# State-space statistics moved to ScalarE, whole products with B in a ring of three, five states weighed by GpSimd, and a multiplied mask

## The reference

```python
h = _layernorm(x) * (1 + ca) + sa
x = x + ga * attention(h)          # 16 heads of 16, causal, linear position bias
h = _layernorm(x) * (1 + cb) + sb
x = x + gb * fp4_ffn(h)            # 704 wide, silu(gate) * up, blocks of 16 rounded to FP4
# second layer, other mod rows
h = _layernorm(x) * (1 + ca) + sa
x = x + ga * state_space(h)
h = _layernorm(x) * (1 + cb) + sb
x = x + gb * experts(h)            # shared and routed low-rank experts
```

```python
xn = layernorm(x) * ln_w + ln_b
x_inner, z = split(xn @ W_in.T)
u = silu(causal_conv4(x_inner) + conv_b)
dt_low, B, C = split(u @ W_x.T)                     # 64, 16, 16
dt = clip(softplus(dt_low @ W_dt.T + b_dt) + DT_MIN, DT_MIN, DT_MAX)
h_t = exp(dt_t * A) * h_(t-1) + (dt_t * u_t) * B_t   # for each channel and state
y_t = sum over states of h_t * C_t, plus u_t * D_param
out = (y * silu(z)) @ W_out.T + x
```

## Time and profile before

| | |
|---|---|
| time before, median of 3 runs | 4210.48 us (4206.35 to 4210.94) |
| profiled execution | 4207.32 us, span 4205.4 us |
| DVE busy | 3592.4 us, 85% of the span |
| PE busy | 3374.6 us, 80% |
| POOL busy | 2620.3 us, 62% |
| ACT busy | 2249.4 us, 53% |

### The profile page before, as it was taken

The page is one execution under the profiler, slowest core; times in us unless marked ns, Lnnn a source line. Parts: engine busy times, 40 slices in busy tenths (PEclk is TensorE's granted clock), DMA queues, the critical chain, the costliest instruction groups (busy, mean ns, idle before and its releaser), DMA issues. The chain is left out here.

```text
span 4205.4 us, 60689 instructions
## 1 busy us (share of the span) xinstructions
PE 3374.6 (80%) x21452; PEld 1522.8 (36%) x21452; DVE 3592.4 (85%) x6348; ACT 2249.4 (53%) x3974; POOL 2620.3 (62%) x2515
## 2 busy tenths in 40 slices
PE   5979999999994999999567777777777777777467
PEld 3623333333332555565222222222222222222166
DVE  5768888888855999999289999999999999999966
ACT  5626666666672333333265665666665565665422
POOL 1102322222222888887188888988889898988823
PEclk8969999999996999999778887888888888887689
DMA  4884565656513111110112222222222222212122
GB/s 146 279 175 67 75 88 67 88 75 82 77 32 87 35 44 47 47 43 26 47 48 52 69 59 62 67 58 50 54 69 60 66 65 56 67 51 52 40 93 83
DMA packets 273931, 299.55 MB, mean 71 GB/s; under 512 B 34559, under 2 KB 204662, under 8 KB 273622
## 3 DMA queue, kind: packets, MB, share of 16 engines
q1 hardware_dynamic: 273630, 295.68, 31.7%
HBM read 210.22 MB, written 84.51 MB: 70 GB/s over the span
## 5 line engine op out<-in xcount | busy, mean ns | idle before, releaser
L1679 POOL TENSOR_TENSOR d_dBu<-d_dtu,d_Bn 128x1024 f32<-128x1024 f32 x512 | 1202.7, 2377 | 157.7 <-DVE d_h L1746 157.5
L1525 ACT ACTIVATE d_dA<-d_dt,d_decay 128x512 f32<-128x512 f32 x1024 | 688.6, 687 | 414.2 <-DVE d_h L1746 412.5
L745 ACT ACTIVATE b_P<-b_pT 128x512 f32<-128x512 f32 (+1 forms) x1120 | 571.4, 576 | 328.8 <-PE b_pT L653 328.5
L1746 DVE TENSOR_TENSOR_SCAN d_h<-d_dA,d_last_h,d_dBu 128x512 f32<-128x512 f32 x512 | 616.9, 1265 | 21.2 <-ACT d_dA L1525 18.2
L1746 DVE TENSOR_TENSOR_SCAN d_h<-d_dA,d_dBu 128x512 f32<-128x512 f32 x512 | 587.1, 1205 | 50.3 <-ACT d_dA L1525 47.9
L775 DVE CUSTOM_DVE_ANT_0 b_pS<-b_pS,mask_qk 128x512 f32<-128x512 f32 (+3 forms) x1024 | 581.2, 618 | 50.1 <-PE b_pS L663 45.1
L663 PE MATMUL b_pS<-KS,QS 99*128 99x512 bf16 (+3 forms) x1536 | 471.4, 339 | 71.7 <-DVE b_Gc L775 47.3
L625 POOL TENSOR_SCALAR_AFFINE_SELECT b_P<-b_P 128x128 f32<-128x128 f32 (+2 forms) x608 | 191.4, 321 | 506.1 <-ACT b_P L745 493.3
L653 PE MATMUL b_pT<-QS,KS 118*128 118x512 bf16 (+3 forms) x1536 | 450.1, 330 | 19.5 <-ACT b_gT L729 16.3
L1753 DVE TENSOR_TENSOR d_h<-d_h,d_C 128x2048 f32<-128x2048 f32 x192 | 434.6, 2263 | 0.5 <-PE d_C L1408 0.5
L1408 PE MATMUL d_C<-d_bc,d_pick 96*128 96x512 bf16 x256 | 118.0, 461 | 359.5 <-DVE d_h L1753 359.2
(11 more groups left out here) (300 smaller groups left out, 5906.5 us busy)
## 6 DMA issues: line engine op xcount, KB each, us to landing
d_Bn<-scratch_bs SPq DMA_DIRECT2D x64, 1024.0 KB, 8.2
scratch_parts<-a_part SPq DMA_DIRECT2D x48, 512.0 KB, 4.1
QS<-scratch_parts SPq DMA_DIRECT2D x192, 128.0 KB, 7.3
KS<-scratch_parts SPq DMA_DIRECT2D x192, 128.0 KB, 7.8
scratch_v<-a_v SPq DMA_DIRECT2D x16, 1024.0 KB, 7.6
V<-scratch_v SPq DMA_DIRECT2D x32, 512.0 KB, 11.7
a_x<-in_L_attn_x_dram SPq DMA_DIRECT2D x16, 512.0 KB, 7.6
scratch_o<-b_O SPq DMA_DIRECT2D x16, 512.0 KB, 10.2
```

The costliest lines, as they stand in the source:

```text
L745: act.activation(t[:, heads[0]:heads[-1] + 1, c * CH:c * CH + w], pT[:, place % RING, 0:len(heads) * w].rearrange("p (h w) -> p h w", w=w) ...
L1525: act.activation(dA[:, m % 2, :], dt[:, c.k % 2, m, :], ACT.Exp, scale=decay[:, m, n:n + 1]).then_inc(dA_d, 1)
L1679: pool.tensor_tensor(dBu[:, n % 2, 2 * j:2 * j + 2, :], dtu[:, c.k % 2, 2 * j:2 * j + 2, :], Bn[:, n // BG % 2, n % BG, :].unsqueeze(1).to ...
L1746: dve.tensor_tensor_scan(h[:, n % HS, m, :], dA[:, m % 2, :], dBu[:, n % 2, m, :], start, ALU.mult, ALU.add).then_inc(scanned, 1)
```

## The change

Four things change.

1. In `attend` the mask of the diagonal blocks is a multiply: the weights, read as 32-bit integers, times `cap`, an integer matrix of ones and zeros that `setup` makes once. The rows that keep the scores out of foreign blocks hold -1024 and no longer -1e30.
2. In `feed_forward` ACT takes the statistics of x2 in two more roles, `s_` and `v_`, 10 and 11 steps back: a Copy that sums, one element scaled to the negated mean over 16, and a Square that sums. They are kept for all 64 tiles, and SP's load of x waits for them besides.
3. In `state_space` the statistics of x by DVE and the four small operations of POOL for them are gone. POOL makes the factors of all 64 tiles at the start, in four operations of 128x64, behind the signal `set_up`. The second layer norm keeps its statistics.
4. POOL makes a product with B whole, 128x2048, into a ring of three states; it waits for all scans of state n-3, and DVE for the whole product. POOL weighs the states 0, 3, 6, 9, 12. B comes two states at a time, so there are 128 transfers of half the size, each as soon as the product two groups before has let its buffer go.

```diff
-                pool.affine_select(out=own, in_=own, compare_op=ALU.is_ge, fill=0.0,
-                                   base=0, pattern=[[0, len(heads)], [-1, P]], channel_multiplier=1).then_inc(p_masked, 1)
+                pool.tensor_tensor(own.bitcast(I32), own.bitcast(I32), K["cap"][:, :].unsqueeze(1).to_broadcast([P, len(heads), P]), ALU.mult).then_inc(p_masked, 1)
...
+                wait(sp, var_d, n.times(1, 1 - XS))
                 sp.dma_start(x[:, n.k % XS, :], xin[bass.ds(n.times(P), P), :]).then_inc(t_in[n.k % 4], 16)
...
+                if v_ is not None:
+                    n = v_.base * U + v_.k
+                    wait(act, sum_d, v_.times(1, 1))
+                    act.activation(K["x2_neg"][:, n:n + 1], x2_sum[:, n % 2, :], ACT.Copy, scale=-1.0 / (16.0 * D)).then_inc(neg_d, 1)
...
                     act.activation(he[:, h_.k % 2, :], he[:, h_.k % 2, :], ACT.Relu, bias=floor[:, :], scale=ROUND).then_inc(hm_d, 1)
+                if v_ is not None:
+                    n = v_.base * U + v_.k
+                    wait(act, neg_d, v_.times(1, 1))
+                    act.activation(unread[:, n % 2, :], x[:, n % XS, :], ACT.Square, bias=K["x2_neg"][:, n:n + 1], scale=1.0 / 16.0, accum_out=K["x2_var"][:, n:n + 1]).then_inc(var_d, 1)
+                if s_ is not None:
+                    n = s_.base * U + s_.k
+                    wait(act, x2_d, s_.times(1, 1))
+                    wait(act, var_d, s_.times(1, -1))
+                    act.activation(unread[:, n % 2, :], x[:, n % XS, :], ACT.Copy, accum_out=x2_sum[:, n % 2, :]).then_inc(sum_d, 1)
...
-POOL_C = (0, 4, 8, 12)
+POOL_C = (0, 3, 6, 9, 12)
...
-HS, BG = 4, 4
+HS, BG, BS = 4, 2, 3
...
+        def product(c, n):
+            return dBu[:, c.times(NS, n) % BS, :, :]
...
+            def spread_next(c, g):
+                if c is not None:
+                    wait(sp, dBu_d, c.times(NS, BG * (g - 1)))
+                    spread_b(c, g)
...
-                for j in range(2):
-                    wait(pool, scanned, c.times(NS * MD, MD * (n - 2) + 2 * j + 2))
-                    pool.tensor_tensor(dBu[:, n % 2, 2 * j:2 * j + 2, :], dtu[:, c.k % 2, 2 * j:2 * j + 2, :],
-                                       Bn[:, n // BG % 2, n % BG, :].unsqueeze(1).to_broadcast([P, 2, CH]), ALU.mult).then_inc(dBu_d, 1)
+                wait(pool, scanned, c.times(NS * MD, MD * (n + 1 - BS)))
+                pool.tensor_tensor(product(c, n), dtu[:, c.k % 2, :, :], Bn[:, n // BG % 2, n % BG, :].unsqueeze(1).to_broadcast([P, MD, CH]), ALU.mult).then_inc(dBu_d, 1)
                 if n - 2 in POOL_C:
                     weigh(c, n - 2)
...
+            pool.tensor_tensor(rstd_x[:, :], K["x2_var"][:, :], eps[:, :], ALU.add).then_inc(sx_step, 1)
+            pool.tensor_tensor(nmr_x[:, :], K["x2_neg"][:, :], sixteen[:, :], ALU.mult).then_inc(sx_step, 1)
+            pool.wait_ge(sx_step, 2)
+            pool.tensor_tensor(rstd_x[:, :], rstd_x[:, :], half[:, :], ALU.pow).then_inc(sx_step, 1)
+            pool.wait_ge(sx_step, 3)
+            pool.tensor_tensor(nmr_x[:, :], nmr_x[:, :], rstd_x[:, :], ALU.mult).then_inc(sx, 1)
...
-                ({15: finish}, {14: step_input}, {3: lambda f: scale_bias(f, 0), 6: shift, 8: lambda f: scale_bias(f, 1)}))
+                ({15: finish}, {14: step_input}, {6: shift, 8: scale_bias}))
...
+                wait(dve, dBu_d, c.times(NS, n + 1))
                 for m in range(MD):
-                    if m % 2 == 0:
-                        wait(dve, dBu_d, c.times(2 * NS, 2 * n + m // 2 + 1))
...
-                 {1: lambda f: stats(f, 0), 4: modulate, 6: lambda f: stats(f, 1), 13: carry}))
+                 {4: modulate, 6: stats, 13: carry}))
```

More of the change, by code:

```diff
@@ L31 @@
 MASKED = -1.0e30
+BELOW = -1024.0
+CAP = 1
 EPS = 1e-5
@@ L1038, in _, with step @@
             pe.wait_ge(w_in, 16)
-            def step(a, e, n_, d, b, h_, q, c, o_):
+            def step(a, e, n_, d, b, h_, q, c, o_, s_, v_):
                 if a is not None:
@@ L1389, in step @@
                 if f is not None and f.k % 2 == 0:
-                    wait_before(sp, x3_d, f.times(1, -2), passed)
+                    wait(sp, x3_d, f.times(1, -2))
                     sp.dma_start(mrow[:, f.k // 2 % 2, GA, :], S["mod"][bass.ds(f.over(2), 1), 1, GA, :].to_broadcast([P, D])).then_inc(g_in[f.k // 2 % 2], 16)
@@ L1555, in normalise @@
                 if 0 in tiles:
-                    wait(act, rs, f.times(2, j + 1))
-                    if j == 1:
+                    if j == 0:
+                        wait(act, sx, 1)
+                        wait(act, x_in, f.times(16, 16))
+                    else:
+                        wait(act, rs, f.times(1, 1))
                         wait(act, h_mul, f.times(1, 1))
@@ L1561, in normalise @@
                 for t in tiles:
-                    last = act.activation(x[:, t, :], src[:, t, :], ACT.Identity, bias=nmr[:, j, t:t + 1], scale=rstd[:, j, t:t + 1])
+                    n = (f.base * U + f.k) * CT + t
+                    bias, scale = (nmr_x[:, n:n + 1], rstd_x[:, n:n + 1]) if j == 0 else (nmr[:, t:t + 1], rstd[:, t:t + 1])
+                    last = act.activation(x[:, t, :], src[:, t, :], ACT.Identity, bias=bias, scale=scale)
                 if CT - 1 in tiles:
@@ new lines, in _, with scale_bias @@
+            pool.tensor_tensor(nmr_x[:, :], K["x2_neg"][:, :], sixteen[:, :], ALU.mult).then_inc(sx_step, 1)
[3 more added lines that the diff above has]
+            pool.tensor_tensor(nmr_x[:, :], nmr_x[:, :], rstd_x[:, :], ALU.mult).then_inc(sx, 1)
+            def scale_bias(f):
+                wait(pool, stat, f.times(2, 2))
+                wait(pool, xn2, f.times(1, 0))
+                pool.tensor_tensor(rstd[:, :], mv[:, :, 1], eps[:, 0:CT], ALU.add).then_inc(rs_step, 1)
+                pool.tensor_tensor(nmr[:, :], mv[:, :, 0], minus[:, :], ALU.mult).then_inc(rs_step, 1)
+                wait(pool, rs_step, f.times(3, 2))
+                pool.tensor_tensor(rstd[:, :], rstd[:, :], half[:, 0:CT], ALU.pow).then_inc(rs_step, 1)
+                wait(pool, rs_step, f.times(3, 3))
+                pool.tensor_tensor(nmr[:, :], nmr[:, :], rstd[:, :], ALU.mult).then_inc(rs, 1)
@@ L1712, in _ @@
             run(pool, unit,
-                ({15: finish}, {14: step_input}, {3: lambda f: scale_bias(f, 0), 6: shift, 8: lambda f: scale_bias(f, 1)}))
+                ({15: finish}, {14: step_input}, {6: shift, 8: scale_bias}))
         @block.vector
         def _(dve):
-            for t, value in ((half, -0.5), (eps, EPS), (minus, -1.0), (growth, GROWTH), (v_max, V_MAX)):
+            for t, value in ((half, -0.5), (eps, EPS), (minus, -1.0), (sixteen, 16.0), (growth, GROWTH), (v_max, V_MAX)):
                 dve.memset(t[:, :], value).then_inc(const, 1)
@@ L1740, in scan @@
                     wait(dve, last_put, c.over(2, NS, n + 1))
+                wait(dve, dBu_d, c.times(NS, n + 1))
                 for m in range(MD):
-                    if m % 2 == 0:
-                        wait(dve, dBu_d, c.times(2 * NS, 2 * n + m // 2 + 1))
                     wait(dve, dA_d, c.times(NS * MD, MD * n + m + 1))
                     start = 0.0 if c.k % 2 == 0 else last_h[:, n, m, :]
-                    dve.tensor_tensor_scan(h[:, n % HS, m, :], dA[:, m % 2, :], dBu[:, n % 2, m, :], start, ALU.mult, ALU.add).then_inc(scanned, 1)
+                    dve.tensor_tensor_scan(h[:, n % HS, m, :], dA[:, m % 2, :], product(c, n)[:, m, :], start, ALU.mult, ALU.add).then_inc(scanned, 1)
             def weigh(c, n):
@@ L1806, in gate_y @@
                 wait(dve, silu_z, e.times(1, 1))
-                wait(dve, dBu_d, e.times(2 * NS, 2 * NS))
+                wait(dve, dBu_d, e.times(NS, NS))
                 dve.tensor_tensor(dtu[:, e.k % 2, :, :], y[:, :, :], z[:, e.k % 2, :, :], ALU.mult).then_inc(yz_d, 1)
```

96 lines of the change are left out of this document (44 added, 52 removed).

## The result

The changed kernel takes 4281.68 us (median of 4 runs, 4279.11 to 4283.25) against 4208.73 us (4 runs) of the kernel before on the same chip: 1.0172 times as long, 95% interval 1.0159 to 1.0185. The prediction was 4270, range 4198 to 4330, slower with a chance of 0.73. The profiled execution took 4281.3 us with a span of 4279.6, that is 74.2 us more than the 4205.4 of before.

The account below looks back on a forecast made before the run. DVE was taken to set the pace of the state-space stage. To 4207.3 us came +33 for its chunks (+2.2 in each of 15), +8 for its head, +22 for the attention: 4270 us, range 4198 to 4330.

Parts of the forecast that it names:

- Attention, +22: Diagonal mask at key tile 3: the integer multiply, priced as float, delays PE about 0.7 us in 32 units, +22 us.
- the multiply costs what the select did: Rival for the attention's mask: the integer multiply is no dearer than the select, total 4248 us; chance 0.12.
- Feed-forward, 0: ACT's two added passes per tile, 1.1 us, lie under 1.6 us of cover before PE needs oT: no cost.
- Head, +8: Start of the state-space stage: the 64-column power takes 10.4 us in series, so the first scan comes 7.7 us later.
- State 3, 1.0 of the statistics' 1.73 comes back: Chunk's turn: without statistics DVE waits for ACT's decay behind PE's convolution, losing 1.0 us a chunk again.
- State 11, +0.9 net: ACT's `grow` and `step_size` delay decays by 1.0 and 0.9 us a chunk; a 1.0 us wait at state 10 goes.
- C of state 12, 0.7: PE sums two states in the turn that projects the gate, so C comes 0.7 us later in a chunk.
- The chunk's end, 2.2: State 15: POOL's whole product, behind a weighing and dtu, makes DVE's scan 2.2 us late in 15 of 16 chunks.
- The port: Three DVE operations with two SBUF inputs lose 0.9 us more a chunk beside POOL's products, now twice as long.
- locked out: Rival: those three DVE operations each wait half a POOL product, 4.8 us more a chunk, total 4328 us; chance 0.07.
- the first rival: DVE's spared work shows in full because POOL delivers state 15's product in time, total 4173 us; chance 0.10.
- the credit for the fifth weighing: State-space chunk: POOL weighs five states, so DVE does one weighing less and is spared 2.26 us a chunk.

Follow-up runs that it names:

- e1: The changed kernel with the select of the diagonal blocks back in place of the integer multiply: 4260.09 us, 1.011 of the kernel before.
- e8: The changed kernel, five states on POOL, with the select, first chunk's factors first, products in halves and dtu in turn 13: 4210.52 us, 1.0004 of the kernel before.
- e10: The changed kernel with four states on POOL, the select, first chunk's factors first, products in halves, dtu in turn 14: 4194.67 us, 0.9956 of the kernel before.
- e9: The changed kernel with four states on POOL, the select, first chunk's factors first, products in halves, dtu in turn 13: 4208.29 us, 1.0002 of the kernel before.
- e6: The changed kernel with DVE taking the statistics of x again and the factors made chunk by chunk: 4280.92 us, 1.016 of the kernel before.
- e3: The changed kernel with each product with B in two halves again, in the ring of three: 4244.16 us, 1.0073 of the kernel before.
- e4: The changed kernel with the next chunk's dtu made in turn 13 in place of 14: 4264.11 us, 1.0124 of the kernel before.
- e5: The changed kernel with POOL weighing four states (0, 4, 8, 12) in place of five: 4242.18 us, 1.0067 of the kernel before.
- e7: The changed kernel with the first chunk's factors made first, the other 60 columns behind that chunk's second statistics: 4270.31 us in one execution.

## Why the prediction was right, and where not

The direction and the range were right, the time 12 us short. Of the 11.2 us between the span's growth (74.2) and the sum of the terms (63), 6.2 are the head, 6.0 the chunks and 1.4 the feed-forward; the attention and the end take 2.4 off. By its own steps:

- **Attention, +22.** Measured 20.7, and e1 gives 20.3 back, 0.63 a unit for 0.7. Price, place and count were right: the float line was the right neighbour for the integer multiply. The earlier trace rows has PE waiting for the mask already (0.36 us), so the whole difference of the prices, 1.27 - 0.634, falls on PE. The rival "the multiply costs what the select did" is out.
- **Feed-forward, 0.** 1.4 us in all. 1.0 of it is there when the first tile comes out, 69.4 us into the stage for 68.4, and the other runs with this stage unchanged scatter there from 68.1 to 69.8; the drain takes 4.1 us in both, so the two more steps cost nothing. The passes cost 0.49 and 0.40 us with 0.19 for each accumulator read, under their cover.
- **Head, +8.** The power took 10.56 us for 10.4, and the first normalisation came 7.8 us later against the stage's start, as worked out. But the first scan came 14.2 us later. The other 6.4 us lie behind it: three of PE's first four projections last 3.75 us and one 1.95, where before the first lasted 3.42 and three 1.95; the granted clock over them is 0.60, and was 0.85. That makes 3.9 us, and the next products of the chain (the first of w_x 6.58 us for 5.28, and one of w_dt 2.04 for 1.09) most of the rest. That step took no account of TensorE's clock. With the power out of the way and the attention as before the head takes 102.6 us in e8 and e10, 103.1 before; in e9 it takes 105.7.
- **State 3, 1.0 of the statistics' 1.73 comes back.** e6: 1.4 comes back. The mechanism was right (decay behind the convolution), the size was read from one row where chunks differ: the wait is none in two of 14 chunks, 1.2 us in seven and 2.5 in five, behind convolutions that end 7.2, 8.7 and 10.3 us after `gate_y` starts (8.9 in every chunk before). The row shown above, 5.87 us at a granted clock of 0.63, is one of the five. The sum of y that ends DVE's wait in front of `gate_y` went the other way by 0.85 us a chunk (2.09 in place of 2.94), which the text did not count.
- **State 4, 0.5.** DVE waits 0.33 at the third decay of state 4 and 0.16 at state 5. Right.
- **State 11, +0.9 net.** At state 11 DVE waits 1.07 and 0.67 us, and 1.24 us at states 9 and 10 are gone: 0.5 net. What the step left out: 0.76 us at state 13 and 0.28 at state 14, where ACT also copies the gate, and on the other side 0.6 us at state 0 and 1.0 at state 7 that are gone.
- **C of state 12, 0.7.** PE makes DVE wait 1.24 us a chunk more, but at states 6, 7 and 14 (its output products, and the sums that free the ring `h`).
- **The chunk's end, 2.2.** 2.29 us, in every chunk; e3 takes it away with the halves, e4 by moving dtu, and e5 keeps 1.84 of it. Right in place, cause and size.
- **The port** (the time that DVE operations lose beside POOL's), **0.9.** 1.6 us: `split_rest` 0.98, `modulate` 0.29, `carry` 0.47, which wasn't named, and `split_lo` 0.14 less. Four states alone take 1.85 us away (e5), halves alone 1.3 (e3). The rival "locked out" (4.8) asked too much. The rule of the Trainium skill that it rests on (SBUF — State Buffer, Who interferes with whom) holds for which instructions collide, the copy included (1.16 us for 0.22); how often they do is a matter of POOL's order, and that no rule gives. The earlier trace rows was read a little too neatly: `split_lo` ended 0.54 us behind POOL's instruction, not with it.
- **Sum, +2.2 a chunk.** 2.61, as 4.50 us more idle time of DVE and 1.89 less busy time; 39.0 us for 33 over the stage.

Two slips of reading change little: the first rival names for POOL's idle time, which stands in the earlier trace rows, and it counts 16 chunks where the sum counts 15 (4 us).

**The step that failed is the credit for the fifth weighing.** The text gave it 2.26 us a chunk and charged 0.5, 0.9 and 0.7 against it, a small gain, and it took the port and the chunk's end as matters of the whole products alone. The runs show no gain in any pair with five and four states: with whole products the chunk takes 120.40 and 117.67 us (after, e5), with halves and dtu in turn 13 117.77 and 117.77 (e8, e9), with halves and dtu in turn 14 117.77 and 116.76 (e3, e10, the last with its short turns; the mask and the power, which also differ there, left the chunk as it was in e1 and e7). And the two changes can't be charged apart. Halves alone (e3) or four states alone (e5) bring the chunk down by 2.63 or 2.73 us, all that it had lost, and both together (e9) bring no more. So these 2.6 us need whole products and a fifth weighing at once. On the port `split_rest` does so too: it takes 2.43 us with both, 1.23 with halves and five states, 1.52 with whole products and four, 1.45 before. `modulate` and the copy go with the fifth weighing alone: 1.78 and 1.16 us with both, 1.72 and 1.09 with halves and five states, 1.21 and 0.32 with four.

**The total was near by luck as well.** In the chunk the text missed some 3 us of charges (port 0.7, state 3 0.4, PE 0.5, the waits at states 13 and 14 0.9, POOL at state 9 0.4) and about as much that went (the sum of y 0.85, state 7 1.0, state 0 0.6, state 11 0.4), and the two nearly cancelled. The attention and the chunk's end were right by their rows.

What stays open: what bounds a chunk at 117.7 us. The kernel before, e3, e5, e8, e9 and the chunks of e10 without a short turn all take 117.67 to 117.79 us on average, while DVE's busy time in a chunk goes from 107.8 (e3) to 110.9 (before). So it isn't DVE's work that sets this time, and the prediction's premise, that what DVE is spared comes off the chunk, fails there. The clock at the turn is a part of it by e10's short turns, but no run holds it still over the whole chunk.

## What to carry to other kernels

POOL, 89% busy over the stage, had no room at the one place where its order puts three long instructions ahead of the one that is waited for: read that place in the order of time before giving it more, and count what every other engine did under the work that is taken away. When two changes meet in one place, take back each alone and both together: here either alone gave back the whole 2.6 us a chunk, so that the two single runs summed would have explained it twice. Work that stands under another engine's chain (the statistics under the convolution) is worth only what sticks out of it, 0.3 of 1.73 us here. And a small serial operation made once for everything (the 64-column power) should be cut so that the first user waits for its own part, with the rest where the engine is idle and not merely behind it.
